# Attention tables made one head further ahead, and later inside a head's step

## The chip, the cores and the metric

The kernel runs on one core of one Trainium2 chip. The metric is the device time of one execution in microseconds (us), lower is better. Before the change three executions took 4916.66, 4945.38 and 4955.33 us; the median is 4945.38 us.

## The reference

One block of a vision tower. The tokens are mixed by an einsum, then an attention with relative position terms is added, then a mixture of eight experts. The change touches the attention alone, for 32 batches (B) of 512 tokens, 16 heads of 16 channels each, 512 heads in all:

```python
scores = jnp.einsum('bhqd,bhkd->bhqk', q, k) / scale
c2p = jnp.einsum('bhqd,hpd->bhqp', q, pos_k)       # each query against 128 distances
c2p = jnp.take_along_axis(c2p, c2p_idx, axis=-1) / scale
p2c = jnp.einsum('bhkd,hpd->bhkp', k, pos_q)       # each key against 128 distances
p2c = jnp.swapaxes(jnp.take_along_axis(p2c, p2c_idx, axis=-1), -1, -2) / scale
scores = scores + c2p + p2c
probs = jax.nn.softmax(scores, axis=-1)
ctx = jnp.einsum('bhqk,bhkd->bhqd', probs, v)
```

## The kernel before, in words

Five stages follow one another: `project` (mixing, norms, q, k, v), `attend`, `output`, `choose` and `experts`. All of `attend` is a pipeline over 512 heads; n is a head's number. One turn of the loop body of an engine is a head's **step**, and it has four **quarters** t = 0 to 3, one for each block of 128 queries. An engine executes its instructions in the order written and waits on semaphores.

The gather by distance is done with a skewed copy in DRAM. For each head TensorE (PE) multiplies the stacked q and k by tables of the distances. These are four **parts** of two products each, `tables` at line 893; there are two PSUM banks, so part 2 waits until part 0 has been copied, and part 3 until part 1 has. ScalarE (ACT) copies each part into `skew_in` (`keep_tables`, line 971). That buffer holds two heads, so the first copy of head n waits until the write of head n-2 has landed (`wait_tables`, line 1071). SyncE (SP) writes the 1 MB block into one of 8 slots of a DRAM ring, `write_tables` at line 768, each row one element further on than the one before. It reads it back with another pitch into `bias`, 0.9 MB (`read_tables`, line 775); the read waits until that head's write has landed, and until the buffer of the head four earlier has been used.

GpSimd (POOL) saves the edge columns of the copied tables (`keep_high`, line 845) and, once the read has landed, fills in the blocks far from the diagonal and the triangles (`part`, line 855). VectorE (DVE) puts in the rest (`fill`, line 1025).

In step n these run, in this order on each engine:

- PE: for each t `scores(n, t)`; in t = 0 a quarter of the `context` product of an earlier group of four heads; `turn(n-2, t)`, which transposes the scores of head n-2; and in t = 0 and 1 two parts each of `tables(n+LEAD)`.
- ACT: for each t `exponent(n-2, t)`; in t = 0 and 1 two parts each of `keep_tables(n+LEAD)`; and at t = 2 of each fourth head `keep_context` (line 987), the copy of a finished context group, ahead of that quarter's exponent.
- DVE: `add_bias(n, 0)`, `fill(n+1)`, then `add_bias` and `lower` by turns.
- POOL: `keep_high(n+LEAD)`, `part(n+NEXT)`.
- SP: `read_tables(n+NEXT)`, a load of two heads' q and k in each second step, `write_tables(n+LEAD)`, now and then a context store or a load of values.

LEAD is 5 and NEXT is 3. Before the loop, PE, ACT, POOL and SP make the tables of the first LEAD heads. Two banks of `m_s` let PE be two quarters of scores ahead of DVE, and two banks of `m_t` two transposes ahead of ACT.

Of the kernel before, what the change touches and what calls it, by code (L numbers as in the profile page):

```python
# [28 lines left out]
NH = 16  # L29
# [26 lines left out]
SW = 2 * S  # L56
EACH = 16
RING = 8
LEAD = 5
NEXT = 3  # L60
SCORED = 4
HIGHS = 8
# [12 lines left out]
def after(eng, sem, count):  # L75

    if not isinstance(count, int) or count > 0:
        eng.wait_ge(sem, count)
# [604 lines left out]
def attend(nc, io, B, ctx, sem, passed, d_tab, d_plain, d_stack, d_v, d_skew, d_ctx):  # L683
# [49 lines left out]
    def origin(hh):  # L733

        return ORIGIN + hh % AHEAD * SLOT

    def turned_at(g, j, k):

        a, c = (k, j) if g % 2 else (j, k)
        return probsT[:, a, c]  # L740
# [13 lines left out]
    with nc.Block() as block:  # L754
        @block.sync
        def _(sp):
            def load_stack(b, g):
                u = g % SR
                sp.dma_start(stack[:, u], d_stack[b, g * SH:(g + 1) * SH].rearrange("h d j x -> (d j) h x")
                             ).then_inc(stack_in[u], 16)  # L760
# [35 lines left out]
            for g in range(1, SR - 1):  # L796
# [4 lines left out]
                load_stack(0, g)  # L801
                if g >= 3 and g - 1 < LEAD:
                    write_tables(g - 1, g - 1, g - 1)
# [5 lines left out]
            def body(b, last):  # L809
                for hh in range(NH):  # L810
# [4 lines left out]
                    if hh % SH == 0:  # L815
                        g = hh // SH + SR - 1
                        if not (last and g >= NS):
                            settled(sp, s_done, QT * n, passed)
                            load_stack(b + g // NS, g % NS)
                    if not (last and hh + LEAD >= NH):  # L820
                        write_tables(n + LEAD, (hh + LEAD) % NH, hh + LEAD)

# [15 lines left out]
        def _(pool):  # L838
# [36 lines left out]
            none = pool.to_reg(0.0)  # L875
            for m in range(LEAD):
                keep_high(m, m)
# [3 lines left out]
            def body(b, last):  # L881
                for hh in range(NH):
                    n = NH * b + hh
                    if not (last and hh + LEAD >= NH):
                        keep_high(n + LEAD, hh + LEAD)
                    if not (last and hh + NEXT >= NH):
# [4 lines left out]
        @block.tensor  # L891
        def _(pe):
            def tables(n, b, hh, part):

                g, w, half = hh // SH, part % 2, part // 2
                if hh % SH == 0 and part == 0:
                    after(pe, stack_in[g % SR], 16 * (NS // SR * b + g // SR + 1))
                after(pe, tab_kept, 4 * n + part - 1)
                for k in range(2):
                    at = (S if w else 0) + (2 * half + k) * P  # L900
                    mm = pe.matmul(m_tab[:, w, k], stack[:, g % SR, hh % SH, at:at + P], tabs[:, w, hh],  # L901
                                   start=True, stop=True)
                mm.then_inc(tab_done, 1)

            def scores(n, hh, t):
                if t == 0:
                    after(pe, filled, 2 * (n + 1))
                after(pe, s_kept, QT * n + t - 1)
                bank = m_s[:, t % 2]
                row = stack[:, hh // SH % SR, hh % SH]  # L910
                pe.matmul(bank[:], row[:, t * P:(t + 1) * P], row[:, S:], start=True, stop=False, skip_group_check=True)  # L911
                near = [k for k in range(QT) if abs(k - t) <= 1]
                for k in near:
                    at = origin(hh) + (OTHER + 2 * t if k > t else RAW[1] + t + k)
                    mm = pe.matmul(bank[:, k * P:(k + 1) * P], bias[:, at], ident[:], start=False,  # L915
                                   stop=(k == near[-1]), is_transpose=True, skip_group_check=True)
                mm.then_inc(s_done, 1)

            def turn(n, hh, k):
                if k == 0:  # L920
                    after(pe, lowered, QT * (n + 1))
                after(pe, turned, QT * n + k - 1)
                for t in range(QT):
                    mm = pe.transpose(m_t[:, k % 2, t * P:(t + 1) * P], scored[:, hh % SCORED, t, k * P:(k + 1) * P],  # L924
                                      ident[:])
                mm.then_inc(turn_done, 1)

            def context(n, b, g, k):

                half = g // (NG // 2)  # L930
                if k == 0:
                    if g % (NG // 2) == 0:
                        after(pe, values_in[half], 16 * (b + 1))
                    after(pe, ctx_kept, NG * b + g)
                after(pe, turned, QT * (n + GH - 1) + k + 1)
                for j in range(GH):
                    mm = pe.matmul(m_ctx[j * CROW:j * CROW + VROW], values[:, half, k, (g * GH + j) % (NH // 2)],  # L937
                                   turned_at(g, j, k), start=(k == 0), stop=(k == QT - 1), skip_group_check=True)
                mm.then_inc(pv_done, 1)

            pe.wait_ge(const_in, 16 * (2 + 2 * SLOTS))
            pe.wait_ge(zeroed_p, 1)
            for m in range(LEAD):
                for part in range(4):
                    tables(m, 0, m, part)

            def body(b, last):
                for hh in range(NH):
                    n, m = NH * b + hh, hh + LEAD
                    for t in range(QT):  # L950
                        scores(n, hh, t)
                        if t == 0 and not early(b, hh, TURN + GH):
                            k, at = (hh - TURN) % GH, hh - TURN - (hh - TURN) % GH - GH
                            context(n - TURN - k - GH, b - 1 if at < 0 else b, at % NH // GH, k)
                        if not early(b, hh, TURN):
                            turn(n - TURN, (hh - TURN) % NH, t)
                        if t < 2 and not (last and m >= NH):
                            for part in (2 * t, 2 * t + 1):
                                tables(n + LEAD, b + m // NH, m % NH, part)

            peeled(pe, B, body, EACH)
            for lag in range(TURN, 0, -1):
                context(HEADS - 2 * GH, B - 1, NG - 2, GH - lag)
                for k in range(QT):
                    turn(HEADS - lag, NH - lag, k)
            for k in range(QT):
                context(HEADS - GH, B - 1, NG - 1, k)

        @block.scalar
        def _(act):  # L970
            def keep_tables(n, par, part):

                u, w, half = par % 2, part % 2, part // 2
                after(act, tab_done, 4 * n + part + 1)
                if part == 0:
                    wait_tables(act, skew_out, n, par)
                    after(act, high_kept, n - 1)
                nc.scalar.activation(skew_in[:, u, w, 2 * half:2 * half + 2], m_tab[:, w], ACT.Identity  # L978
                                     ).then_inc(tab_kept, 1)

            def exponent(n, hh, k):
                after(act, turn_done, QT * n + k + 1)
                after(act, pv_done, n - GH + 1)
                nc.scalar.activation(turned_at(hh // GH, hh % GH, k), m_t[:, k % 2], ACT.Exp, scale=SCALE  # L984
                                     ).then_inc(turned, 1)

            def keep_context(b, g):
                after(act, pv_done, GH * (NG * b + g + 1))
                after(act, ctx_out, 16 * (NG * b + g))
                nc.scalar.activation(ctx_sb[:, g % 2], m_ctx[:], ACT.Identity).then_inc(ctx_kept, 1)  # L990

            load_tabs(act, 1)
            for m in range(LEAD):
                for part in range(4):
                    keep_tables(m, m, part)

            def body(b, last):
                for hh in range(NH):
                    n, m = NH * b + hh, hh + LEAD
                    for t in range(QT):  # L1000
                        if t == 2 and hh % GH == KEPT % GH and not early(b, hh, KEPT):
                            keep_context(b, (hh - KEPT) // GH)
                        if not early(b, hh, TURN):
                            exponent(n - TURN, (hh - TURN) % NH, t)
                        if t < 2 and not (last and m >= NH):
                            for part in (2 * t, 2 * t + 1):
                                keep_tables(n + LEAD, m, part)

            peeled(act, B, body, EACH)
            for lag in range(TURN, 0, -1):  # L1010
                for k in range(QT):
                    exponent(HEADS - lag, NH - lag, k)
            for g in (NG - 2, NG - 1):
                keep_context(B - 1, g)
# [813 lines left out]
```

## Time and profile before

| | |
|---|---|
| median of three runs | 4945.38 us |
| profiled execution, its own time | 4949.42 us |
| its span | 4947.7 us |
| mean granted TensorE clock | 0.958 |
| busy: PE, DVE, ACT, POOL | 91%, 71%, 54%, 38% |
| first and last `add_bias` of the attention start at | 958.75 and 4127.25 us |

The span is the time between the first and the last instruction of the profiled execution. The attention takes about two thirds of it, and the 512 steps follow one another at an almost even rate, so 0.01 us in each step is 5 us of the whole. PE's busy time is that of overlapping products with modelled ends. The share of the DMA engines is a mean over 16 of them.

### The profile page before, as it was taken

What the parts mean: (1) busy time and instruction counts of PE and PEld (TensorE: products, weight loads), DVE (VectorE), ACT (ScalarE), POOL (GpSimd) and SP (SyncE); (2) the same over time, 40 slices, a digit from 0 to 9 for tenths busy, and PEclk for the clock granted to TensorE, in tenths of its full rate; (3) what the DMA queues carried; (4) which work ended last, traced back from release to release, by engine and by line L of the source; (5) the groups of instructions that cost most, each with busy time, mean ns of one, the idle gap of its engine ahead of it and who ended that gap; (6) DMA issues with size and microseconds to landing.
All of it is one profiled execution on the core that took longest, in us unless ns stands there. A gap on an engine that the chain in (4) does not pass through costs nothing. (4 is left out here: it accounts for less than half of the span.)

```text
span 4947.7 us, 91672 instructions
## 1 busy us (share of the span) xinstructions
PE 4503.2 (91%) x29893; PEld 3225.0 (65%) x30324; DVE 3496.9 (71%) x9091; ACT 2689.6 (54%) x5075; POOL 1862.1 (38%) x4431
## 2 busy tenths in 40 slices
PE   6999999599999999999999999999999997883699
PEld 5777777366666666666666666666666665773566
DVE  3333333388888888888888888888888886776511
ACT  1222222277777777777667676767676664441111
POOL 1222222244444444444444444444444442330032
PEclk9999999799999999999999999999999998885599
DMA  5888888899999999999999999999999996662033
GB/s 169 279 285 275 278 286 276 292 382 382 379 388 387 390 378 375 373 378 376 369 376 377 376 372 373 378 373 383 371 377 368 373 369 205 215 207 82 3 96 82
DMA packets 684020, 1540.36 MB, mean 311 GB/s; under 512 B 50211, under 2 KB 286163, under 8 KB 683475
## 3 DMA queue, kind: packets, MB, share of 16 engines
q1 hardware_dynamic: 674646, 1523.26, 85.1%
q0 software_dynamic: 6144, 8.52, 1.0%
q8 instruction: 217, 3.56, 0.3%
q10 hardware_dynamic: 2816, 3.41, 0.2%
q14 instruction: 197, 1.61, 0.1%
HBM read 753.82 MB, written 781.21 MB: 310 GB/s over the span
## 5 line engine op out<-in xcount | busy, mean ns | idle before, releaser
L984 ACT ACTIVATE a_probsT<-a_ps_m_t 128x512 f32<-128x512 f32 x2048 | 1223.8, 605 | 828.0 <-PE a_ps_m_t L924 828.0
L1046 DVE CUSTOM_DVE_ANT_1 a_scored<-a_ps_m_s,a_bias 128x512 f32<-128x512 f32 x2048 | 1393.1, 680 | 311.0 <-PE a_ps_m_s L915 302.0
L924 PE MATMUL a_ps_m_t<-a_ident,a_scored 128*128 128x128 f32 x8192 | 1257.7, 276 | 0.5 <-ACT a_probsT L984 0.5
L924 PEld LDWEIGHTS a_ps_m_t<-a_ident,a_scored 128*128 128x128 f32 x8192 | 935.2, 141 | 433.2 <-DVE a_scored L1053 427.8
L978 ACT ACTIVATE a_skew_in<-a_ps_m_tab 128x512 f32<-128x512 f32 x2048 | 1124.2, 612 | 163.8 <-DMA d_skew<-a_skew_in 126.9
L1053 DVE TENSOR_SCALAR a_scored<-a_scored,a_top_of 128x512 f32<-128x512 f32 x2048 | 1075.1, 545 | 0.0
L870 POOL TENSOR_SCALAR_AFFINE_SELECT a_bias<-a_bias 128x128 f32<-128x128 f32 (+2 forms) x2560 | 1004.8, 419 | 35.1
L861 POOL COPY a_bias<-a_high 128x128 f32<-128x128 f32 (+1 forms) x1024 | 358.4, 380 | 1679.8 <-DMA a_bias<-d_skew 1679.8
L915 PE MATMUL a_ps_m_s<-a_ident,a_bias 128*128 128x128 f32 x5120 | 895.7, 273 | 22.1 <-issue 0.7
L901 PE MATMUL a_ps_m_tab<-a_tabs,a_stack 128*128 128x256 bf16 x4096 | 711.5, 276 | 159.9 <-ACT a_skew_in L978 87.4
L915 PEld LDWEIGHTS a_ps_m_s<-a_ident,a_bias 128*128 128x128 f32 x5120 | 690.1, 141 | 177.5 <-issue 1.4
L1031 DVE COPY_PREDICATED a_bias<-a_ps_m_past,a_high 128x384 f32<-128x384 int32 x1024 | 543.5, 582 | 142.7 <-POOL a_bias L870 116.2
L911 PE MATMUL a_ps_m_s<-a_stack 128*128 128x512 bf16 x1639 | 622.8, 380 | 0.8 <-DVE a_top_of L1046 0.6
L901 PEld LDWEIGHTS a_ps_m_tab<-a_tabs,a_stack 128*128 128x128 bf16 x4096 | 331.2, 98 | 391.0 <-ACT a_skew_in L978 338.7
L937 PE MATMUL a_ps_m_ctx<-a_probsT,a_values 128*17 128x512 f32 x4096 | 538.4, 598 | 1.2 <-ACT a_ctx_sb L990 1.2
L177 PE MATMUL p_ps_m_h<-p_mix,p_xt 128*128 128x256 f32 x2048 | 467.8, 382 | 23.3 <-DVE t_stats L279 23.3
L177 PEld LDWEIGHTS p_ps_m_h<-p_mix,p_xt 128*128 128x128 f32 x2048 | 389.9, 192 | 115.7 <-issue 44.5
L911 PEld LDWEIGHTS a_ps_m_s<-a_stack 128*128 128x128 bf16 x2048 | 200.7, 98 | 15.4 <-issue 2.4
L586 POOL TENSOR_TENSOR p_rest_q<-p_full_q,p_part_q 128x512 f32<-128x512 f32 x64 | 90.4, 1413 | 306.5 <-ACT p_part_q L535 306.5
L649 DVE CAST p_part_q<-p_rest_q 128x512 bf16<-128x512 f32 x64 | 27.3, 427 | 233.5 <-POOL p_rest_q L586 233.5
L609 DVE BATCH_NORM_STATS2 p_stats<-p_h_sb 128x6 f32<-128x256 f32 x128 | 47.9, 416 | 173.5 <-ACT p_h_sb L516 173.5
L1046 DVE DVE_READ_ACCUMULATOR2_ANT a_top_of<- 128x1 f32 x2048 | 164.7, 80 | 0.0
(195 smaller groups left out, 3566.8 us busy)
## 6 DMA issues: line engine op xcount, KB each, us to landing
d_skew<-a_skew_in SPq DMA_DIRECT2D x512, 1024.0 KB, 9.5
a_bias<-d_skew SPq DMA_DIRECT2D x512, 896.0 KB, 8.6
a_stack<-d_stack SPq DMA_DIRECT2D x256, 512.0 KB, 9.0
p_xt<-in_xT SPq DMA_DIRECT2D x31, 2048.0 KB, 10.4
d_stack<-p_extra SPq DMA_DIRECT2D x64, 512.0 KB, 3.2
d_ctx<-a_ctx_sb SPq DMA_DIRECT2D x128, 256.0 KB, 9.9
d_stack<-p_part_q SPq DMA_DIRECT2D x64, 384.0 KB, 2.8
d_stack<-p_part_k SPq DMA_DIRECT2D x64, 384.0 KB, 3.4
```

The costliest lines, as they stand in the source:

```text
L177: mm = pe.matmul(m_h[:, t], xt[:, u, k, t * P:(t + 1) * P], mix[:, k], start=(k == 0), stop=(k == ND * HC - 1))
L870: nc.gpsimd.affine_select(blocks(r + out[0], (out[1], count)), blocks(r + of, (2, count)), pattern=[[0, count], [-sign, P]], base=0, chann ...
L901: mm = pe.matmul(m_tab[:, w, k], stack[:, g % SR, hh % SH, at:at + P], tabs[:, w, hh], start=True, stop=True)
L911: pe.matmul(bank[:], row[:, t * P:(t + 1) * P], row[:, S:], start=True, stop=False, skip_group_check=True)
L915: mm = pe.matmul(bank[:, k * P:(k + 1) * P], bias[:, at], ident[:], start=False, stop=(k == near[-1]), is_transpose=True, skip_group_check ...
L924: mm = pe.transpose(m_t[:, k % 2, t * P:(t + 1) * P], scored[:, hh % SCORED, t, k * P:(k + 1) * P], ident[:])
L937: mm = pe.matmul(m_ctx[j * CROW:j * CROW + VROW], values[:, half, k, (g * GH + j) % (NH // 2)], turned_at(g, j, k), start=(k == 0), stop=( ...
L978: nc.scalar.activation(skew_in[:, u, w, 2 * half:2 * half + 2], m_tab[:, w], ACT.Identity).then_inc(tab_kept, 1)
L984: nc.scalar.activation(turned_at(hh // GH, hh % GH, k), m_t[:, k % 2], ACT.Exp, scale=SCALE).then_inc(turned, 1)
L1031: nc.vector.copy_predicated(blocks(r + at, (step, QT - 1)), m_past[:, w].unsqueeze(1).to_broadcast([P, QT - 1, P]), high[:, v, w].unsqueez ...
L1046: nc.vector.tensor_tensor_reduce(split(scored[:, hh % SCORED, t]), split(m_s[:, t % 2]), extra, 1.0, -3.0e38, ALU.add, ALU.max, top_of[:, ...
L1053: nc.vector.tensor_scalar(at, at, top_of[:, hh % 2, t:t + 1], None, ALU.subtract).then_inc(lowered, 1)
```

## The change

`LEAD` goes from 5 to 6. The tables, their copies, their saved edges and their write are those of head n+6 in step n, and the part before the loop makes six heads' tables. In the loop bodies of PE and ACT the two parts of the table products, and their two copies, move from quarters t = 0 and 1 to quarters t = 2 and 3. The amount of work, the buffers and NEXT stay.

```diff
--- before.py
+++ after.py
@@ -56,7 +56,7 @@
 SW = 2 * S
 EACH = 16
 RING = 8
-LEAD = 5
+LEAD = 6
 NEXT = 3
 SCORED = 4
 HIGHS = 8
@@ -954,8 +954,8 @@
                             context(n - TURN - k - GH, b - 1 if at < 0 else b, at % NH // GH, k)
                         if not early(b, hh, TURN):
                             turn(n - TURN, (hh - TURN) % NH, t)
-                        if t < 2 and not (last and m >= NH):
-                            for part in (2 * t, 2 * t + 1):
+                        if t >= 2 and not (last and m >= NH):
+                            for part in (2 * t - 4, 2 * t - 3):
                                 tables(n + LEAD, b + m // NH, m % NH, part)
 
             peeled(pe, B, body, EACH)
@@ -1002,8 +1002,8 @@
                             keep_context(b, (hh - KEPT) // GH)
                         if not early(b, hh, TURN):
                             exponent(n - TURN, (hh - TURN) % NH, t)
-                        if t < 2 and not (last and m >= NH):
-                            for part in (2 * t, 2 * t + 1):
+                        if t >= 2 and not (last and m >= NH):
+                            for part in (2 * t - 4, 2 * t - 3):
                                 keep_tables(n + LEAD, m, part)
 
             peeled(act, B, body, EACH)
```

On PE this is one head's step of the fourth batch onwards, where the pipeline is full (L911 and L915 are `scores`, L937 `context`, L924 `turn`, L901 `tables`, four products in a row of two parts). Before:

```order
L937 MATMUL a_ps_m_ctx<-a_probsT,a_values 17x512 x4
L924 MATMUL a_ps_m_t<-a_ident,a_scored 128x128 x4
L901 MATMUL a_ps_m_tab<-a_tabs,a_stack 128x256 x4
L911 MATMUL a_ps_m_s<-a_stack 128x512
L915 MATMUL a_ps_m_s<-a_ident,a_bias 128x128 x3
L924 MATMUL a_ps_m_t<-a_ident,a_scored 128x128 x4
L901 MATMUL a_ps_m_tab<-a_tabs,a_stack 128x256 x4
L911 MATMUL a_ps_m_s<-a_stack 128x512
L915 MATMUL a_ps_m_s<-a_ident,a_bias 128x128 x3
L924 MATMUL a_ps_m_t<-a_ident,a_scored 128x128 x4
```

And now:

```order
L937 MATMUL a_ps_m_ctx<-a_probsT,a_values 17x512 x4
L924 MATMUL a_ps_m_t<-a_ident,a_scored 128x128 x4
L911 MATMUL a_ps_m_s<-a_stack 128x512
L915 MATMUL a_ps_m_s<-a_ident,a_bias 128x128 x3
L924 MATMUL a_ps_m_t<-a_ident,a_scored 128x128 x4
L911 MATMUL a_ps_m_s<-a_stack 128x512
L915 MATMUL a_ps_m_s<-a_ident,a_bias 128x128 x3
L924 MATMUL a_ps_m_t<-a_ident,a_scored 128x128 x4
L901 MATMUL a_ps_m_tab<-a_tabs,a_stack 128x256 x4
L911 MATMUL a_ps_m_s<-a_stack 128x512
L915 MATMUL a_ps_m_s<-a_ident,a_bias 128x128 x2
L924 MATMUL a_ps_m_t<-a_ident,a_scored 128x128 x4
```

Between the two halves of the tables there used to stand the scores of t = 1, with three blocks of bias, and a transpose; now there stand the scores of t = 3, with two blocks, and a transpose.

On ACT, around a context copy (L984 is `exponent`, L978 `keep_tables`, L990 `keep_context`), before:

```order
L978 ACTIVATE a_skew_in<-a_ps_m_tab 128x512 x2
L984 ACTIVATE a_probsT<-a_ps_m_t 128x512
L978 ACTIVATE a_skew_in<-a_ps_m_tab 128x512 x2
L990 ACTIVATE a_ctx_sb<-a_ps_m_ctx 128x512
L984 ACTIVATE a_probsT<-a_ps_m_t 128x512 x3
```

And now:

```order
L984 ACTIVATE a_probsT<-a_ps_m_t 128x512 x2
L990 ACTIVATE a_ctx_sb<-a_ps_m_ctx 128x512
L984 ACTIVATE a_probsT<-a_ps_m_t 128x512
L978 ACTIVATE a_skew_in<-a_ps_m_tab 128x512 x2
L984 ACTIVATE a_probsT<-a_ps_m_t 128x512
L978 ACTIVATE a_skew_in<-a_ps_m_tab 128x512 x2
```

The context copy used to come behind the last copy of a table; now it comes before the first, with one exponent between them. On SP only the rows before the loop and at its end differ: one more write ahead of the loop, one fewer in it.

## Rows read from the trace of the kernel before

**Rows 1.** Windows of the span: start:end, length, each engine's busy us (instructions), PEclk, DMA share, GB/s.
```profile
1600.00:1700.00 100.00, 98.04 (x758) 69.70 (x771) 89.04 (x234) 71.79 (x138) 47.57 (x135) 1.00 1.02 391
3700.00:3800.00 100.00, 94.24 (x719) 65.90 (x732) 84.88 (x222) 68.72 (x130) 45.82 (x128) 1.00 1.01 370
```

**Rows 2.** Windows of L1031 alone (`fill`, two per head): length, busy (count), PEclk, DMA share, GB/s.
```profile
1000.00:1500.00 500.00, 87.11 (x164) 1.00 1.01 383
...
2000.00:4000.00 2000.00, 339.68 (x640) 1.00 1.01 375
```

**Rows 3.** DMA issues, 1500 to 4000 us: transfer, queue, count, KB each, median us to landing.
```profile
d_skew<-a_skew_in SPq DMA_DIRECT2D x402, 1024.0 KB, 9.6
a_bias<-d_skew SPq DMA_DIRECT2D x402, 896.0 KB, 8.6
```

**Rows 4.** Waits, 1500 to 4000 us: who waits <- for whom: us in total, times, longest.
```profile
DVE a_bias L1031 <- POOL a_bias L870: 95.1, 129, 1.7
ACT a_skew_in L978 <- DMA d_skew<-a_skew_in: 94.7, 215, 1.4
```

**Rows 5.** Waits of SP's queue, 1500 to 4000 us.
```profile
SPq L782 <- DMA d_skew<-a_skew_in: 748.1, 394, 3.4
```

**Rows 6.** Timeline of one step: start, length, engine, line, operation, tiles [idle before <-releaser].
```profile
2405.70 0.10 PEld L911 LDWEIGHTS a_ps_m_s<-a_stack 128*128 128x128 bf16 x1
...
2407.32 0.66 PE L924 MATMUL a_ps_m_t<-a_ident,a_scored 128*128 128x128 f32 x4
...
2408.01 0.60 ACT L984 ACTIVATE a_probsT<-a_ps_m_t 128x512 f32<-128x512 f32 x1 [1.41 <-PE a_ps_m_t L924]
...
2408.50 1.08 ACT L978 ACTIVATE a_skew_in<-a_ps_m_tab 128x512 f32<-128x512 f32 x2
...
2408.79 0.60 PE L924 MATMUL a_ps_m_t<-a_ident,a_scored 128*128 128x128 f32 x4
...
2409.23 0.81 PE L901 MATMUL a_ps_m_tab<-a_tabs,a_stack 128*128 128x256 bf16 x4
...
2409.64 0.11 PEld L901 LDWEIGHTS a_ps_m_tab<-a_tabs,a_stack 128*128 128x128 bf16 x2 [0.31 <-ACT a_skew_in L978]
...
2410.41 0.60 PE L924 MATMUL a_ps_m_t<-a_ident,a_scored 128*128 128x128 f32 x4
...
2411.28 0.60 PE L924 MATMUL a_ps_m_t<-a_ident,a_scored 128*128 128x128 f32 x4
...
2411.61 0.10 PEld L911 LDWEIGHTS a_ps_m_s<-a_stack 128*128 128x128 bf16 x1
```

**Rows 7.** The same timeline: SP's issues and the bias work of that step.
```profile
2405.17 0.36 SPq L772 DMA_DIRECT2D d_skew<-a_skew_in  x1
...
2407.51 0.52 SPq L782 DMA_DIRECT2D a_bias<-d_skew  x1
...
2408.11 1.06 DVE L1031 COPY_PREDICATED a_bias<-a_ps_m_past,a_high 128x384 f32<-128x384 int32 x2
...
2410.80 0.64 POOL L861 COPY a_bias<-a_high 128x128 f32<-128x128 f32 x2 [3.17 <-DMA a_bias<-d_skew]
...
2411.39 1.75 POOL L870 TENSOR_SCALAR_AFFINE_SELECT a_bias<-a_bias 128x128 f32<-128x128 f32 x4
```

**Rows 8.** Timeline of SP and of ACT when the attention starts.
```profile
940.57 2.95 SPq L772 DMA_DIRECT2D d_skew<-a_skew_in  x2
...
944.71 1.09 ACT L978 ACTIVATE a_skew_in<-a_ps_m_tab 128x512 f32<-128x512 f32 x2 [1.57 <-DMA d_skew<-a_skew_in]
...
956.00 1.09 ACT L978 ACTIVATE a_skew_in<-a_ps_m_tab 128x512 f32<-128x512 f32 x2 [5.66 <-DMA d_skew<-a_skew_in]
```

**Rows 9.** Groups by line, 1500 to 4000 us: the context copy: busy us, mean ns | idle before.
```profile
L990 ACT ACTIVATE a_ctx_sb<-a_ps_m_ctx 128x512 f32<-128x512 f32 x101 | 65.4, 648 | 0.0
```

**Rows 10.** Timeline of DVE: the first and the last `add_bias` of the attention.
```profile
958.75 0.69 DVE L1046 CUSTOM_DVE_ANT_1 a_scored<-a_ps_m_s,a_bias 128x512 f32<-128x512 f32 x1 [4.04 <-PE a_ps_m_s L915]
...
4127.25 0.68 DVE L1046 CUSTOM_DVE_ANT_1 a_scored<-a_ps_m_s,a_bias 128x512 f32<-128x512 f32 x1
```

## The prediction

> **What bounds the kernel now.** I read the windows first. In the attention the DMA share is 1.01 or 1.02 in every window, and TensorE is granted its full clock, the 2.4 GHz level, at 1.00 [rows 1]. So both the rings and PE, busy 94 to 98 us in 100, may be the bound. The rate moves between 370 and 391 GB/s with the same share, and the work goes with it. A share of one is therefore no proof of a fixed rate.
>
> How long is a step? `fill` runs twice per head. 164 in 500 us make 6.10 us a head early on, 640 in 2000 us make 6.25 us later [rows 2]. Over the whole attention it is (4127.25 - 958.75) / 512 = 6.19 us [rows 10].
>
> What would a step be without DMA? I looked in the timeline for one that shows no wait for a transfer, and found it between the first score products of two heads: 2405.70 to 2411.61, or 5.91 us [rows 6]. PE runs through it without a pause but for one: part 3 of the tables waits 0.31 us for ACT's copy of part 1. That is the **floor** of the compute. It leaves 6.19 - 5.91 = 0.28 us a step, 143 us of the span, as the price of transfers that come late.
>
> The waits say which. DVE's `fill` waits for POOL 95.1 us in some 402 steps, and POOL is late because the read landed late; ACT's first copy waits 94.7 us for a write to land [rows 4]. Each is 0.24 us a step, and together they cover the 0.28. Behind both stands SP: the read waits for the landing of its own head's write practically every time, 394 of some 402, 1.9 us each [rows 5].
>
> **The change: what LEAD 6 gives.** First the chain before. SP issues the write of head n+5 at 2405.17, in step n. It lands after 9.6 us, the read after another 8.6 us [rows 3]. POOL's work on it runs from 2410.80 over the copies and four triangles to 2411.39 + 1.75 = 2413.14, and a fifth triangle is a quarter of that 1.75 more: 2.8 us [rows 7]. The sum is 21.0 us. The `fill` at 2408.11 is that of step n+1 [rows 7]; the one that wants this head stands in step n+4, three steps on, at 2408.11 + 3 x 6.19 = 2426.68, which is 21.5 us after the write's issue. The median transfer has 0.5 us to spare, so a late one is felt at once.
>
> With six ahead, and the write half a step later, the write has landed before the read's turn comes, and the read is freed of it. What holds the read then is SP's own order. `write_tables(n+6)` waits for the copies that end step n, and `read_tables(n+4)` stands behind it. The last copy of a table should now end some 1.5 us after PE has begun the next scores at 2405.70 [rows 6], so I take 2407.5 for both. That is where the read goes out at its earliest now [rows 7]. Head n+4 is wanted by the `fill` two steps after the one at 2408.11, 0.6 + 2 x 6.19 = 13.0 us later; less 2.8 for POOL, the read may take 10.2 us. It takes 8.6 now. Behind a write that was issued 0.4 us earlier it takes longer. From below: the first write of the attention, with nothing ahead of it, was issued at 940.57 and released ACT at 944.71, so 4.1 us [rows 8]; 0.92 MB more at 375 GB/s are 2.4 us, together 6.5. From above: the queue that makes the write's 4.1 into 9.6 stays as it is, then 6.5 + 5.5 = 12.0. I take 9.3, the middle, with 0.9 us to spare instead of 0.5. By this the wait of `fill` roughly halves. The write must be home before the copy two steps on: 2 x 6.19 less the burst of copies, 2408.50 to about 2411.06 or 2.6 us, as before, but now no read has been issued just ahead of it. It should take 1 or 2 us less, and ACT's wait mostly goes. I put what is left of the 0.28 at 0.10 us, between 0 and 0.28.
>
> The Trainium skill, in "DMA: Bandwidth & Descriptors", "Measured" and "Anatomy of one DMA", gives 2.0 us plus the bytes at 436 GB/s for a transfer alone. An estimate from it is 4.4 us for the write; the trace's 4.1 agrees. The same page says ("Issuing engines are not separate DMA queues") that all transfers share the same 16 engines, which speaks against this change: a write and a read that go out together are served one after the other.
>
> **What the new quarters cost.** The copy chain of ACT does not get shorter: from the end of turn 0 at 2407.98 an exponent from 2408.01, two copies until 2409.58, and part 3's weights at 2409.64, 1.66 us [rows 6]. PE's work in the meantime does. It used to be two parts, scores with three blocks and a transpose, from 2407.98 to the end of turn 1 at 2409.39: 1.41 us. In the new place it is two parts (0.43), scores with two blocks and a transpose (end of turn 2 at 2411.01 to end of turn 3 at 2411.88: 0.87), so 1.30 us. The pause before part 3 grows from 0.31 to **0.42 us**, by 0.11 a step.
>
> Once in four heads the context copy, 0.648 us [rows 9], stands between exponents 1 and 2. It used to come after all copies, where nobody waited. Exponent 1 (0.60) and the copy make 1.25 us after the end of turn 1. Turn 2 now ends 0.98 us after turn 1, the 1.41 of above less two parts. So exponent 2, both copies and part 3 come 0.27 us later in each fourth step: 0.07 a step. Between 0 and 0.16, if all of the copy shows.
>
> The new floor is 5.91 + 0.11 + 0.07 = 6.09 us.
>
> **What costs nothing.** POOL's `keep_high` now waits for copies that end just as it comes to them; behind it stands `part`, for whose read POOL stands idle 3.17 us [rows 7], and that idle time covers it. DVE keeps its order. It needs the tables of nothing before POOL does, and with fewer table products early in the step PE brings it the scores of t = 1 and 2 earlier, while it has half a microsecond to spare in a step. The clock is at its upper level throughout and PE's idle share stays within what the window of 370 GB/s shows [rows 1], so I cost it at nothing.
>
> **Before the loop** a sixth head's tables come ahead of the first scores. Such a head waited up to 5.7 us for a write [rows 8]. But the old loop met the same tables in its first step and had its PE wait there, so only what PE did before them moves back: I take +2 us, between 0 and 6. At the end one more step runs without table products; two parts more or less are 0.4 us there, so -1 for all four.
>
> **The sum.** 512 x (6.09 + 0.10 - 6.19) = 0, plus 1: 1 us. Against the profiled execution's 4949.42 us (span 4947.7) that is 4950; the median of the runs shown is 4 us below it. 4950 less 4 is 4946; with the upper halves of the bounds the larger ones I round up to **4948 us**, against the median of 4945.38.
>
> **Rivals.**
>
> *The rings are the bound.* Per head they move 375 x 6.25 = 2.34 MB whatever the order, and their share is one. If the engine that lands last is never idle, more room only makes its queue longer, and the step stays at 6.19 to 6.25: from no change to 0.06 x 512 = 31 us more. For it: the share. Against it: 391 GB/s in one window. This too is no change; I give it 0.20, and my own forecast 0.36.
>
> *Faster: the late transfers go and little is lost.* The step falls to 5.91 + 0.11 = 6.02 with the context copy hidden: -0.17 x 512 = -87, so 4945 - 87 = 4858 us. For it: SP's 1.9 us before each read are gone, and the waits of rows 4 hang on that. Against it: the write stays in front of the read. The Trainium skill's "HBM Reference" ("Specifications") has a core that streams alone at about 425 GB/s; by that a head's bytes would be an estimate of 5.5 us, below the floor, and this rival's way would be open. No window here is above 391. Chance 0.19.
>
> *Slower: the floor goes up and the waits stay.* The mechanism is the pair on SP. If the read keeps the whole queue, 12.0 us against the 10.2 it may take, `fill` waits in more steps than before, and at t = 3 PE now comes to its scores without the two parts of tables that used to give DVE time. The point from which it decides is a read of 10.2 us to landing. With all of the 0.28 us kept on the new floor the step is 6.37: +0.18 x 512 = +92, so 5037 us. Chance 0.25.
>
> **The range.** A change of 1% (49 us) is about what can be told here. Faster by more: 0.19. Slower by more: 0.25. Within: 0.56. The range of 8 in 10 takes in the likeliest case, 4920 to 4985, and most of the two others, from 4875 to 5025.
>
> **What would show it.** SP's wait of the read for its write should vanish, and a wait for ACT's copies stand in front of nearly each write. The read should take more than 8.6 us to land, about 9.3, and the write less than 9.6. The PE wait of L901 for L978 should be about 0.42 us in a quiet step. DVE's wait for POOL should fall to near 0.12 us a step and ACT's for the write to near nothing. The step in the middle should be 6.2 us. I am wrong if the read's time to landing is above 10.2 us, or if quiet steps still take 5.9 us.

## The result and the profile after

The changed kernel takes 4878.64 us (median of four, 4873.04 to 4883.87) against 4939.41 us before (median of four, the three shown and one more). The ratio is 0.988 with a 95% interval of 0.9838 to 0.9922. It is faster by 61 us, where the prediction had no change, 4948 us. Here and below a ratio and its interval leave out runs that lie more than 1.5% above the fastest of the same kernel. The profiled execution took 4879.16 us, its span is 4877.4 us, 70.3 us less than before.

The windows (columns as in [rows 1]) show both stretches at nearly the same rate, where the kernel before had 391 and 370 GB/s:

```profile
1600.00:1700.00 100.00, 98.47 (x766) 68.30 (x764) 86.39 (x229) 71.68 (x138) 46.24 (x136) 1.00 1.02 387
3700.00:3800.00 100.00, 98.52 (x768) 68.50 (x760) 85.87 (x229) 71.32 (x136) 45.52 (x132) 1.00 1.02 389
```

`fill` alone in windows, as in [rows 2]:

```profile
1000.00:1500.00 500.00, 88.39 (x166) 1.00 1.01 385
...
2000.00:4000.00 2000.00, 352.81 (x662) 1.00 1.02 386
```

662 in 2000 us are 6.04 us a head instead of 6.25. The share is 1.02 and was 1.01. A head's bytes are the same (386 x 6.04 and 375 x 6.25 are both 2.3 MB), so GB/s here are only the step told in another way. Neither they nor the share say what bounds the step.

DMA issues (as [rows 3]), then the waits (as [rows 4] and [rows 5]), all from 1500 to 4000 us:

```profile
d_skew<-a_skew_in SPq DMA_DIRECT2D x413, 1024.0 KB, 7.7
a_bias<-d_skew SPq DMA_DIRECT2D x413, 896.0 KB, 9.5
```

```profile
DVE a_bias L1031 <- POOL a_bias L870: 258.2, 303, 2.7
PEld a_ps_m_tab L901 <- ACT a_skew_in L978: 135.9, 372, 0.4
...
ACT a_skew_in L978 <- DMA d_skew<-a_skew_in: 0.2, 1, 0.2
```

```profile
SPq L772 <- ACT a_skew_in L978: 1591.1, 413, 6.3
```

SP no longer waits for a write before a read at all: that row of [rows 5], 748.1 us, has no successor. The write lands sooner (7.7 against 9.6 us) and the read later (9.5 against 8.6). ACT's wait for the write is gone. DVE's wait for POOL is not: it has grown from 95.1 to 258.2 us, 0.63 us a step, in a kernel that is faster. It is idle time that DVE had at another place, in the wait of `add_bias` for PE's scores (the kernel before, then now):

```profile
DVE a_scored L1046 <- PE a_ps_m_s L915: 238.2, 314, 2.0
```

```profile
DVE a_scored L1046 <- PE a_ps_m_s L915: 43.3, 201, 0.4
```

Together the two waits were 0.83 us a step and are 0.73. DVE now comes to `fill` earlier in the step, and waits there:

```profile
2411.88 1.07 DVE L1031 COPY_PREDICATED a_bias<-a_ps_m_past,a_high 128x384 f32<-128x384 int32 x2 [0.94 <-POOL a_bias L870]
```

It was ready at 2410.94, 1.6 us after the first score weights of that step (2409.37, below). In the kernel before it was 2.4 us, 2408.11 after 2405.70 [rows 6] [rows 7].

PE, the busiest engine, shows where the late transfers had reached it. Its weight loads for the tables wait for ACT's copies, in the kernel before (1500 to 4000 us):

```profile
PEld a_ps_m_tab L901 <- ACT a_skew_in L978: 260.6, 631, 1.5
```

That was 0.65 us a step, 0.34 more than the 0.31 of the quiet step; now it is the 135.9 us shown above, 0.33 a step. The 631 waits in some 402 steps are 229 more than one a step, about as many as ACT's 215 waits for a write to land [rows 4]. So before, a late write held ACT's copies, and these held PE.

A quiet step, from the first scores of one head to those of the next (timeline, as [rows 6]):

```profile
2403.35 0.10 PEld L911 LDWEIGHTS a_ps_m_s<-a_stack 128*128 128x128 bf16 x1
...
2406.98 0.60 PE L924 MATMUL a_ps_m_t<-a_ident,a_scored 128*128 128x128 f32 x4
...
2407.62 0.60 ACT L984 ACTIVATE a_probsT<-a_ps_m_t 128x512 f32<-128x512 f32 x1 [0.38 <-PE a_ps_m_t L924]
...
2408.11 1.08 ACT L978 ACTIVATE a_skew_in<-a_ps_m_tab 128x512 f32<-128x512 f32 x2
...
2408.29 0.60 PE L924 MATMUL a_ps_m_t<-a_ident,a_scored 128*128 128x128 f32 x4
...
2409.24 0.11 PEld L901 LDWEIGHTS a_ps_m_tab<-a_tabs,a_stack 128*128 128x128 bf16 x2 [0.37 <-ACT a_skew_in L978]
...
2409.37 0.10 PEld L911 LDWEIGHTS a_ps_m_s<-a_stack 128*128 128x128 bf16 x1
```

It takes 6.02 us, 0.11 more than the 5.91 of [rows 6]. The profile gives the pause before part 3 as 0.37 us, where 0.42 had been forecast; counted from the end of the transpose before it, 0.35 us (2408.89 to 2409.24) against 0.25 (2409.39 to 2409.64), it has grown by 0.10. From the end of turn 2 (2407.58) to the weights of part 3 (2409.24) are 1.66 us, the same chain of an exponent and two copies.

The first and the last `add_bias` (as [rows 10]):

```profile
964.94 0.69 DVE L1046 CUSTOM_DVE_ANT_1 a_scored<-a_ps_m_s,a_bias 128x512 f32<-128x512 f32 x1 [10.31 <-PE a_ps_m_s L915]
...
4055.45 0.68 DVE L1046 CUSTOM_DVE_ANT_1 a_scored<-a_ps_m_s,a_bias 128x512 f32<-128x512 f32 x1
```

They lie 3090.5 us apart, 6.04 us a step against 6.19, and the first comes 6.2 us later than it did. 3168.5 - 3090.5 = 78.0 us gained in the steps, 6.2 lost before them, leave 71.8 us, and the span shows 70.3.

### The profile page after: what moved, and what is told of

It reads as the page before. It is cut to its first block and busy times, and to the rows that moved or that the text cites. A ratio compares the mean times of both kernels' runs of the same rounds, so it can differ in the third digit from the quotient of the medians.

```text
span 4877.4 us, 92103 instructions
## 1 busy us (share of the span) xinstructions
PE 4504.8 (92%) x30324; PEld 3209.8 (66%) x30324; DVE 3455.7 (71%) x9091; ACT 2682.0 (55%) x5075; POOL 1818.4 (37%) x4431
## 5 line engine op out<-in xcount | busy, mean ns | idle before, releaser
L984 ACT ACTIVATE a_probsT<-a_ps_m_t 128x512 f32<-128x512 f32 x2048 | 1231.5, 602 | 874.2 <-PE a_ps_m_t L924 872.4
L924 PE MATMUL a_ps_m_t<-a_ident,a_scored 128*128 128x128 f32 x8192 | 1257.1, 276 | 0.5 <-ACT a_probsT L984 0.5
L924 PEld LDWEIGHTS a_ps_m_t<-a_ident,a_scored 128*128 128x128 f32 x8192 | 934.2, 141 | 433.2 <-DVE a_scored L1053 328.3
L978 ACT ACTIVATE a_skew_in<-a_ps_m_tab 128x512 f32<-128x512 f32 x2048 | 1123.8, 614 | 53.8 <-PE a_ps_m_tab L901 34.9
L1053 DVE TENSOR_SCALAR a_scored<-a_scored,a_top_of 128x512 f32<-128x512 f32 x2048 | 1021.2, 519 | 0.0
L870 POOL TENSOR_SCALAR_AFFINE_SELECT a_bias<-a_bias 128x128 f32<-128x128 f32 (+2 forms) x2560 | 994.6, 416 | 35.1
L861 POOL COPY a_bias<-a_high 128x128 f32<-128x128 f32 (+1 forms) x1024 | 369.8, 391 | 1632.5 <-DMA a_bias<-d_skew 1632.5
L915 PE MATMUL a_ps_m_s<-a_ident,a_bias 128*128 128x128 f32 x5120 | 894.7, 273 | 0.0
L915 PEld LDWEIGHTS a_ps_m_s<-a_ident,a_bias 128*128 128x128 f32 x5120 | 691.2, 141 | 174.1 <-issue 0.8
L911 PE MATMUL a_ps_m_s<-a_stack 128*128 128x512 bf16 x2048 | 778.5, 380 | 27.7 <-DVE a_top_of L1046 26.0
L1031 DVE COPY_PREDICATED a_bias<-a_ps_m_past,a_high 128x384 f32<-128x384 int32 x1024 | 545.5, 585 | 342.7 <-POOL a_bias L870 314.2
L901 PE MATMUL a_ps_m_tab<-a_tabs,a_stack 128*128 128x256 bf16 x4096 | 702.4, 276 | 86.3 <-DMA a_ident<-in_ident 31.6
L937 PE MATMUL a_ps_m_ctx<-a_probsT,a_values 128*17 128x512 f32 x4096 | 538.3, 598 | 1.2 <-ACT a_ctx_sb L990 1.2
L901 PEld LDWEIGHTS a_ps_m_tab<-a_tabs,a_stack 128*128 128x128 bf16 x4096 | 327.9, 98 | 283.3 <-ACT a_skew_in L978 187.5
L911 PEld LDWEIGHTS a_ps_m_s<-a_stack 128*128 128x128 bf16 x2048 | 200.2, 98 | 69.6 <-DVE a_top_of L1046 56.0
## 6 DMA issues: line engine op xcount, KB each, us to landing
a_stack<-d_stack SPq DMA_DIRECT2D x256, 512.0 KB, 10.2
```

The costliest lines, as they stand in the source:

```text
L870: nc.gpsimd.affine_select(blocks(r + out[0], (out[1], count)), blocks(r + of, (2, count)), pattern=[[0, count], [-sign, P]], base=0, chann ...
L1031: nc.vector.copy_predicated(blocks(r + at, (step, QT - 1)), m_past[:, w].unsqueeze(1).to_broadcast([P, QT - 1, P]), high[:, v, w].unsqueez ...
L1053: nc.vector.tensor_scalar(at, at, top_of[:, hh % 2, t:t + 1], None, ALU.subtract).then_inc(lowered, 1)
```

## The experiments

All are compared with the kernel before on the same chip. Its median over these runs lay between 4912 and 4934 us.

**The two halves of the change.** Six ahead alone:

```diff
-LEAD = 5
+LEAD = 6
```

> Tables six heads ahead, but still made in quarters 0 and 1. The read no longer waits for its write, yet it still goes out ahead of the next write in the ring. Theory A (what cost 0.28 us a step before was ACT waiting for the write to land, because a read and a stack load stood in the ring just ahead of the write): the write still takes 9 us or more, ACT still waits, the step stays between 6.10 and 6.20 us, 4900 to 4950 us. Theory B (what cost it was the read held back until the write had landed, and so a late fill on DVE): the step falls to the old floor of 5.91 plus 0.03, 512 x 0.25 = 128 us less than before, about 4815 us, and DVE's wait for POOL is near zero.

It took 4823.53 us, ratio 0.979 (0.9719 to 0.9861). The move to quarters 2 and 3 alone:

```diff
-if t < 2 and not (last and m >= NH):
-    for part in (2 * t, 2 * t + 1):
+if t >= 2 and not (last and m >= NH):
+    for part in (2 * t - 4, 2 * t - 3):
```

> Tables five heads ahead, but made in quarters 2 and 3. The write and the next read go out back to back at the end of a step, and the read of this head comes one step later, when the write has hardly landed. Theory A: the write goes out into an emptier ring, lands in about 7.7 us, ACT does not wait; the time is near that of the full change, 4870 to 4900 us. Theory B: the read must wait 1.5 us for its write again and lands near the limit of 10.2 us; the fill is late in most steps and the time is 4940 us or more.

It took 4883.71 us, ratio 0.9919 (0.9884 to 0.9955). So theory B had the first right and theory A the second: each half by itself makes the kernel faster, and together they are worth less than six ahead alone, about what the move alone is worth. The waits of six ahead alone, and its `fill` in windows:

```profile
DVE a_bias L1031 <- POOL a_bias L870: 27.6, 52, 1.1
ACT a_skew_in L978 <- DMA d_skew<-a_skew_in: 9.3, 20, 1.3
```

```profile
2000.00:4000.00 2000.00, 357.19 (x674) 1.00 1.02 390
```

Both waits are nearly gone and the step is 5.93 us, close to the floor of 5.91. The move alone runs at the other floor; its median time to landing is 7.4 us for the write, and SP still waits for it, but briefly, 0.86 us a step where it was 1.9:

```profile
SPq L782 <- DMA d_skew<-a_skew_in: 355.6, 298, 2.5
```

```profile
2000.00:4000.00 2000.00, 352.87 (x662) 1.00 1.02 386
```

**The floors.** If the transfers are made lighter, what is left is compute. In both kernels only 64 of the 1024 columns of q and k are loaded in the loop, `stack[:, u, :, 0:64]`, 32 KB instead of 512.

> The kernel before, with the stack loads in the loop cut from 512 KB to 32 KB (all but 64 of 1024 columns are left stale, so heads after the 16th use old q and k). A head then moves 2.1 MB instead of 2.34. If the 0.28 us above the quiet step of 5.91 us are all due to transfers, the step falls to 5.91 to 5.95 us: 512 x 0.26 = 133 us less, about 4805 us. If part of them is something else, it falls less.

> The changed kernel with the same cut of the stack loads. Its quiet step is 6.02 us and its mean step 6.04; if the floor of the compute is what bounds it, the cut brings 10 to 15 us, about 4865 us, and it is slower than the kernel before with the same cut by 0.11 x 512 = 56 us. If the rings bind it, it falls by 30 us or more.

4810.23 us and 4864.9 us. The order turns round: with light transfers the changed kernel is 55 us slower. In the traces 4.6 us of that lie ahead of the first `add_bias` (963.58 against 958.94), and the steps are (3986.41 - 958.94) / 512 = 5.91 us and (4042.28 - 963.58) / 512 = 6.01 us, 0.10 apart. `fill` in a window, first of the kernel before with light loads, then of the changed one:

```profile
1000.00:1500.00 500.00, 90.61 (x170) 1.00 0.99 353
```

```profile
1000.00:1500.00 500.00, 88.22 (x166) 1.00 0.98 347
```

The share falls to 0.99 and 0.98. In the kernel before with light loads the write lands in 5.3 us, and both waits of [rows 4] are gone from its list. The 0.28 us a step were due to transfers, as the prediction had it. From the changed kernel the light loads take only 0.02 us a step (6.036 to 6.013), although its share was 1.02: a share above one does not say that the transfers are the bound.

**Why the floor rose.** Six ahead with the tables in quarters 1 and 2, so that scores with three blocks stand between the halves again:

```diff
-if t < 2 and not (last and m >= NH):
-    for part in (2 * t, 2 * t + 1):
+if t in (1, 2) and not (last and m >= NH):
+    for part in (2 * t - 2, 2 * t - 1):
```

> Six heads ahead, tables in quarters 1 and 2. Between the two halves stand the scores of t = 2, with three blocks of bias as in the old place, and a transpose. If the 0.11 us of the move come from the shorter work between the halves, the quiet step is 5.91 us and the time is that of six-ahead alone, 4815 to 4835 us. If they come from being late in the step (the copies run against the next step's exponents, the context copy stands in front), the quiet step is between 5.91 and 6.02 and the time 4840 to 4870 us.

4834.35 us, ratio 0.9811 (0.974 to 0.9882), within the first range and 11 us above six ahead alone. The pause is back at its old length:

```profile
2404.87 0.11 PEld L901 LDWEIGHTS a_ps_m_tab<-a_tabs,a_stack 128*128 128x128 bf16 x2 [0.31 <-ACT a_skew_in L978]
```

So the 0.11 us are the missing block of scores, not the lateness in the step.

**Whether the pause can go.** Parts 0 and 1 in quarter 0, 2 in quarter 1, 3 in quarter 2 (`((0, 1), (2,), (3,))[t]`), six ahead; and the same with light loads:

> Six heads ahead, tables spread as parts 0 and 1 in quarter 0, part 2 in quarter 1, part 3 in quarter 2. PE no longer waits 0.31 us for ACT's copy, so the floor of the compute is 5.60 us. If the compute still binds, the step falls to 5.7 us or less: 4700 us or so. If the rings bind at the 389 GB/s that the tables-six-ahead kernel moved, 2.34 MB a head take 6.0 us, and the time stays at 4810 to 4835 us with ACT or DVE waiting for transfers again. The burst of copies is also 1 us longer, which leaves the write 1 us less to land; if that decides, it is slower than 4824 us, 4840 to 4880.

> Tables spread over three quarters, six heads ahead, with the stack loads cut to 32 KB (heads after the 16th use old q and k). If the three-quarter kernel was held by the rings, the step falls from 5.95 to the floor of the compute without the pause, 5.60 to 5.70 us: 4670 to 4710 us. If something else holds it at 5.95, nothing changes: 4815 to 4830 us.

4829.11 us, ratio 0.981 (0.9739 to 0.9881): no better than six ahead alone. With light loads 4712.01 us. The first kernel's `fill`, and then the second's:

```profile
2000.00:4000.00 2000.00, 356.83 (x672) 1.00 1.02 389
```

```profile
1000.00:1500.00 500.00, 93.15 (x176) 1.00 1.01 366
```

That is 5.95 and 5.68 us a head. With the pause taken away the transfers are the bound, 2.3 MB in 5.95 us, and ACT waits for writes again (79.2 us from 1500 to 4000). The two bounds lie within 0.05 us of each other.

**Which wait had cost the 0.28 us.** First DVE's. POOL gets 0.54 to 0.58 us more per head between the landing and its work:

```diff
+nc.gpsimd.memset(idle[:], 0.0)          # 128 x 512, at the start of part()
```

> The kernel before, with a memset of 512 columns on POOL between the landing of each head's read and the work on it (some 0.5 us more before the bias is ready). If the late fill is what costs in the kernel before, each late step grows by most of it: 0.2 us a step or more, 5010 us or more. If ACT's wait for the write alone costs and DVE makes up for a late fill, less than 0.1 us a step: 4910 to 4960 us.

> The changed kernel with the same memset. DVE waits 0.62 us a step for POOL there already, while the quiet step stays 6.02 us. If DVE makes up for a late fill in its spare 0.64 us, the wait grows to 1.0 us or more and the time by less than 50 us (below 4930). If the spare time is used up, the whole of it goes to the step: 0.3 us or more, above 5030 us.

> Six heads ahead, tables in quarters 0 and 1, with the same memset. DVE waits only 0.07 us a step for POOL there, since the read goes out as soon as its buffer is free. The memset should be hidden almost entirely: 4825 to 4850 us. If it is not, the fill is nearer to late than the waits show.

Before: 4905.91 us, ratio 0.9967 (0.9913 to 1.0021), no difference. DVE's wait for POOL doubled all the same:

```profile
DVE a_bias L1033 <- POOL a_bias L872: 188.5, 315, 2.2
```

The changed kernel went to 4911.1 us, 32 more than without; six ahead alone to 4834.96, 11 more. DVE's wait is 0.47 us a step in the first and 0.72 in the second. A late `fill` is free at 0.5 us a step in the kernel before, and costs something from 0.6 on, about where DVE's spare time ends. DVE's wait was not the price. Then ACT's, by a third buffer of copied tables (`skew_in` with 3 in place of 2, indexed by `n % 3`):

> The kernel before with three buffers of copied tables instead of two, and nothing else: ACT's first copy then waits for the write of three heads earlier, and the 0.24 us a step of ACT's waits for a write to land go. SP still holds each read back until its own write has landed. If ACT's wait is the price of late transfers in the kernel before, the step falls to 5.93 to 6.00 us and the time to 4800 to 4850 us. If the price lies in the read that is held back, or in the rate of the rings in that order, little changes: 4890 us or more.

It is slower: 4970.8, 5002.58 and 5011.45 us and once 5060.44, ratio 1.0127 (1.0044 to 1.021). ACT's wait is gone, and this stands in its place (waits, DMA issues, SP's waits, `fill`):

```profile
DVE a_bias L1031 <- POOL a_bias L870: 448.7, 383, 3.4
```

```profile
d_skew<-a_skew_in SPq DMA_DIRECT2D x395, 1024.0 KB, 11.2
a_bias<-d_skew SPq DMA_DIRECT2D x395, 896.0 KB, 8.9
```

```profile
SPq L782 <- DMA d_skew<-a_skew_in: 1177.9, 395, 5.0
```

```profile
2000.00:4000.00 2000.00, 335.64 (x630) 1.00 1.01 368
```

Writes go out as soon as they can, stand in a longer queue (11.2 us), and the read, which waits for that landing, is later still. The chain is now 11.2 + 8.9 + 2.8 = 22.9 us against the 21.5 of the prediction, and the step is the longest of all, 6.35 us. PE's waits have moved with it:

```profile
PEld a_ps_m_tab L901 <- ACT a_skew_in L978: 122.5, 395, 0.3
PEld a_ps_m_s L911 <- DVE a_top_of L1046: 122.2, 201, 2.4
```

It waits for the copies 0.31 us a step, as in the quiet step, and for DVE another 0.31. So DVE's wait had cost nothing in the kernel before, while ACT's was the one by which late transfers reached PE. But it cannot be taken off alone: without it the lateness goes to `fill`, 1.14 us a step, more than DVE has to spare.

**Why the transfers came late.** In the kernel before each read goes out at the moment a write has landed, that is when all 16 of its parts have been counted; in that trace the last comes 3.3 us after the first (median). Two kernels, six ahead with the tables in quarters 0 and 1, delay the read by about as much, without need. One ties it to the landing of the next head's write, the other to DVE's first `add_bias` of the step:

```diff
+w = min(n + 1, HEADS - 1)
+settled(sp, skew_out[w % 2], 16 * (w // 2 + 1), passed)
```

```diff
-settled(sp, s_kept, QT * (n - AHEAD + 1), passed)
+settled(sp, s_kept, QT * (n - AHEAD + 1) + (n >= AHEAD - 1), passed)
```

> Six heads ahead, tables in quarters 0 and 1, two buffers, but each read now also waits until the write of the next head has landed, as in the kernel before a read went out at the moment a write landed. The data needs none of it: the read's own write landed long ago. Theory L (tying the read to the landing of a write, that is to the slowest of the 16 engines, leaves the others short of work, and the rings then move less): 375 to 380 GB/s, a step of 6.15 us or more, 4900 to 4960 us. Theory C (the chain of write, read and POOL was too long for the fill, and nothing else): the chain is short here, so 4820 to 4860 us with 388 GB/s or more.

> The same kernel with each read held until DVE has done the first add_bias of the step, about 1.6 us later than its buffer comes free, and no wait for a landing. Theory L: the time stays near that of six-ahead alone, 4820 to 4850 us, with 388 GB/s, since the read's time is fixed by the compute. If lateness of the read by itself costs, whatever it is tied to, it is as slow as the one held by a write, 4880 us or more.

The first took 4941.86 us, ratio 1.0039 (1.0004 to 1.0074), its profiled execution 4926: all that six ahead had brought is gone, and theory C is out. The second took 4852.8 us, 0.9854 (0.9788 to 0.992), 3 us outside what theory L allowed and 27 under the other. SP's waits (L78 is the helper `settled`, which waits) and `fill`, first of the one held by a write:

```profile
SPq L78 <- DMA d_skew<-a_skew_in: 1010.8, 388, 4.7
```

```profile
2000.00:4000.00 2000.00, 345.87 (x652) 1.00 1.02 381
```

and of the one held by DVE:

```profile
SPq L78 <- DVE a_top_of L1046: 912.5, 416, 3.9
```

```profile
2000.00:4000.00 2000.00, 353.75 (x669) 1.00 1.02 389
```

The waits are alike, 2.5 and 2.2 us a head, and the medians lie 89 us apart, 5.5 of them ahead of the first `add_bias` (969.88 against 964.38). The mere delay costs 29 us against six ahead alone. This speaks for the tie to a landing, but the two kernels differ in one thing more, which was not tested by itself: how far the read goes out ahead of the next write. SP's timeline, held by a write and then held by DVE:

```profile
2416.05 0.53 SPq L784 DMA_DIRECT2D a_bias<-d_skew  x1
...
2418.62 0.36 SPq L772 DMA_DIRECT2D d_skew<-a_skew_in  x1
```

```profile
2413.81 0.53 SPq L782 DMA_DIRECT2D a_bias<-d_skew  x1
...
2417.01 0.36 SPq L772 DMA_DIRECT2D d_skew<-a_skew_in  x1
```

In the median of some 400 steps it is 2.6 us when held by a write, as in the kernel before, 3.1 us when held by DVE and 4.6 us with six ahead alone. The write behind it lands in 9.4, 8.8 and 8.5 us, and ACT waits for it 58.5, 19.3 and 9.3 us. With the third buffer on the kernel before it was 1.4 us, and the write took 11.2. The steps, from the first to the last `add_bias`, are 6.12, 5.97 and 5.94 us. From 4.6 to 3.1 us the step grows by 0.03 us, from 3.1 to 2.6 by 0.15, so the distance alone would have to act very unevenly; nor does it fix the landing, which is 9.1 us at 4.6 us with the three buffers below. And a tie by itself need not cost: the move alone keeps one in 298 of some 414 steps, with its reads 4.4 us ahead of the next write, and runs within 0.03 us of its floor.

That the quick engines run short of work while the slowest one finishes is partly borne out by the packet records of the traces. Fewer than 14 packets were in flight in 3.2% of the time before, 2.2% when held by a write, 0.6% when held by DVE and 0.6% with six ahead alone. But between the kernel before and six ahead alone their mean number grows only from 16.2 to 16.4, 1.3%, while the bytes per us grow by some 4%. The rest is that packets take less long, those of the reads 151 ns in the mean instead of 159, and why they do no run shows.

**The best of both.** Six ahead, quarters 0 and 1, three buffers:

> Six heads ahead, tables in quarters 0 and 1, and three buffers. ACT waits for a write only 0.02 us a step in the two-buffer kernel, so the steady steps have nothing to gain: 5.95 us. Before the loop the sixth head's tables no longer wait for the write of the fourth but of the third, 3 to 6 us of the 6.3 that the first scores came later. About 4818 us, between 4810 and 4830.

4811.53 us (4808.86 to 4812.51), ratio 0.9771 (0.9725 to 0.9818). It beats both kernels. The gain over six ahead alone is 12 us, where about 6 were expected, all of them ahead of the loop. By the traces the first `add_bias` comes 2.7 us earlier, and the step is (3988.08 - 962.29) / 512 = 5.91 us against (4005.95 - 965.03) / 512 = 5.94, 15 us in all; what follows the attention happened to take 8 us longer in that execution. The buffer that harmed the kernel before helps this one, whose reads are not tied to the writes.

## Why the prediction was wrong

*The floor, 5.91 + 0.11 from the shorter work between the halves.* Right: 6.02 in the trace, and confirmed from both sides by the light loads (0.10 us a step) and by quarters 1 and 2.

*The context copy, 0.07 a step.* Wrong, it is zero. I added the lengths of an exponent and of the copy, 0.60 + 0.65 = 1.25 us, and compared with 0.98 on PE. Around such a copy the changed kernel shows starts at 2400.61, 2401.11 and 2401.59:

```profile
2400.61 0.60 ACT L984 ACTIVATE a_probsT<-a_ps_m_t 128x512 f32<-128x512 f32 x1 [0.38 <-PE a_ps_m_t L924]
...
2400.96 0.60 PE L924 MATMUL a_ps_m_t<-a_ident,a_scored 128*128 128x128 f32 x4
...
2401.11 0.59 ACT L990 ACTIVATE a_ctx_sb<-a_ps_m_ctx 128x512 f32<-128x512 f32 x1
...
2401.59 0.60 ACT L984 ACTIVATE a_probsT<-a_ps_m_t 128x512 f32<-128x512 f32 x1
```

These instructions follow one another after 0.50 and 0.48 us although each is on record for 0.6, so the two take 0.98, just what PE takes, and the next exponent starts 0.03 us after the end of turn 2 at 2401.56.

*What is left of the late transfers, 0.10 a step.* This is the step that failed most: 6.04 - 6.02 leaves 0.02. The prediction read the two waits of [rows 4], 0.24 us each, as the price, and asked how much room each would have. Two waits of 0.24 are 0.48 us, more than the 0.28 to be explained, so not both could be the price in full. It got the read's landing nearly right (9.3 against 9.5 us, limit 10.2), expected DVE's wait to halve, and saw it grow to 0.63 us, at a cost of 0.02 us at most. The room was too large: 10.2 us reckoned with a `fill` 2.4 us into the step, and DVE now comes to it after 2.1 us in the quiet step (2405.41 after 2403.35) and 1.6 us in the next, which leaves 9.9 and 9.4 us for a read of 9.5. The 0.10 priced what would be left of DVE's wait, and that wait has no price of this size. POOL slowed by more than half a microsecond left the kernel before where it was. ACT's wait, which did reach PE, went to nothing as forecast, and with it the cost. What the lateness itself hung on was the row that the prediction called only "behind both": SP's 748.1 us [rows 5], the read that goes out when a write has landed, shortly ahead of the next one. Without that wait, six ahead alone is 0.03 us from its floor; with 355.6 us of it left the move alone is 0.03 us from its own; put back on six ahead it costs 0.18 us a step (6.12 against 5.94). How much of this is the tie and how much the place of the read stays open.

*The signs.* The prediction would call itself wrong at a read above 10.2 us or a quiet step of 5.9 us. Neither came (9.5 and 6.02), so they did not test the term that failed. That a write and a read which go out together slow each other, which it held against the change, did show in the read (9.5 against 8.6 us), and cost little.

*The terms together.* 0.07 + 0.08 = 0.15 us a step too much, 77 us. Before the loop I had 2 us and it was 6.2, the upper bound; this took 4 back. Against the profiled execution the sum had been 4950, and 4950 - 77 + 4 = 4877, where 4879 was measured. The mechanism was that of the rival "faster" (5.91 + 0.11, context copy hidden, -87 us), which had a chance of 0.19; the late transfers left 0.02 us a step more than it allowed.

*The half-step move.* The prediction did not ask what six ahead would give without it. It would have been 5.91 + 0.02, and the measured difference between the two is 4878.64 - 4823.53 = 55 us.

*The rival "the rings are the bound".* Wrong for this change, since the same bytes went through in 6.04 us a step, and right for what comes next: the kernel that has no pause stays at 5.95 us, and at 5.68 with lighter loads.

## What to carry to other kernels

Read the price of late transfers from the waits of the engine that bounds the kernel, here PE, and not from those of the engines before it: DVE's wait grew from 0.24 to 0.63 us a step while the kernel became faster. A wait that ends before its engine is needed is free, so before it is priced it should be lengthened or removed on the chip, one alone; and one that is removed can come back in another place, as ACT's did in `fill`. Where a queue issues a transfer only after another has landed, try what the kernel does when it need not. With the same bytes in each step, GB/s say no more than the step does, and a share of busy time of one does not say that the transfers bind; making them lighter does. And of two edits made together, ask for each what it gives without the other.

## What was not expected of the hardware

- At a share of 1.01 to 1.02 the same bytes moved at 368, 375, 381, 386, 389 and 390 GB/s. Lighter loads took 0.28 us off a step at 1.01 and 0.02 off one at 1.02, so the share told neither the rate nor whether the transfers were the bound.
- The 16 parts of a 1 MB write landed over 3.3 us (median from the first to the last) in the kernel before, and over 1.0 us there with the light loads.
- The runs of the kernel before (4888 to 4970 us), with its third buffer (4971 to 5060) and of the one held by a write (4926 to 4979) scatter by more than 1%; those of six ahead with three buffers lie between 4808.86 and 4812.51 us, those of the move alone, whose reads wait for a write only briefly, between 4878 and 4888.
- An exponent, the context copy and the next exponent, 128 x 512 each, start 0.50 and 0.48 us apart on ACT, while each is shown with 0.59 or 0.60.
